# A linear-attention and expert layer on one core: second gate and router with fewer TensorE passes, a norm moved, eight blocks a body

## What is computed

```python
x = x + attention(layernorm(x))          # x: (2, 8192, 512) fp32, 16384 tokens in all
x = x + experts(layernorm(x))

# attention, 16 heads of 32, chunks of 64 tokens
q, k, v = h @ Wq + bq, h @ Wk + bk, h @ Wv + bv
gate  = sigmoid(silu(h @ Wg1 + bg1) @ Wg2 + bg2)     # Wg1: (512, 16), Wg2: (16, 512)
alpha = 0.9 * gate + 0.1
intra = softmax(causal(q k^T / sqrt(32))) v          # within a chunk
inter_t = q_t S;   S = alpha_t * S + k_t v_t^T       # a state per head, token by token
out = intra + inter

# experts, 64 of them, top 8 per token, 256 slots each, and one shared expert
probs = softmax(h @ router_w.T); w = top8(probs) / sum
out = sum_e w_e * (silu(h @ w_gate[e]) * (h @ w_up[e])) @ w_down[e]
    + (silu(h @ sg) * (h @ su)) @ ws_down
```

## Time and profile before

| | |
|---|---|
| median of 3 runs | 4751.03 us |
| the profiled execution | 4743.73 us, span 4741.9 us |
| TensorE busy, matmuls | 4469.1 us (94%), 74544 instructions |
| VectorE busy | 3521.0 us (74%) |
| ScalarE busy | 2271.8 us (48%) |
| POOL busy | 1333.6 us (28%) |
| granted TensorE clock, mean | 0.983 |
| DMA | 358.52 MB, mean 76 GB/s |

### The profile page before, as it was taken

One profiled execution on the slowest core, in us unless ns is written; L12 is line 12 of the kernel. 1 busy time (PEld: TensorE's weight loads), 2 busy tenths in 40 slices (PEclk: granted clock), 3 DMA queues, 4 the chain that ended last, 5 costly groups with the idle time before them and its releaser, 6 DMA issues. The chain is left out here.

```text
span 4741.9 us, 183468 instructions
## 1 busy us (share of the span) xinstructions
PE 4469.1 (94%) x74544; PEld 3903.7 (82%) x74544; DVE 3521.0 (74%) x7639; ACT 2271.8 (48%) x7475; POOL 1333.6 (28%) x1272
## 2 busy tenths in 40 slices
PE   6999999999999999999999999999999959999998
PEld 5888888888888888888888888888888859999998
DVE  5777777777777777777777777777777768888887
ACT  4444444444444444444444444444444436666665
POOL 2111111111111111111112121212111146666666
PEclk9999999999999999999999999999999979999999
DMA  2000000001000000000000000000000069999997
GB/s 65 31 31 31 31 33 28 36 31 36 31 31 31 31 31 31 31 31 31 31 31 31 31 31 31 31 31 34 28 35 31 31 193 269 267 266 267 269 270 194
DMA packets 195054, 358.52 MB, mean 76 GB/s; under 512 B 16736, under 2 KB 92896, under 8 KB 194352
## 3 DMA queue, kind: packets, MB, share of 16 engines
q1 hardware_dynamic: 160848, 269.47, 16.8%
q0 software_dynamic: 33632, 79.73, 7.6%
HBM read 243.87 MB, written 107.50 MB: 74 GB/s over the span
## 5 line engine op out<-in xcount | busy, mean ns | idle before, releaser
L583 ACT ACTIVATE PR<-PR,MX 128x64 f32<-128x64 f32 x2048 | 682.6, 334 | 808.1 <-DVE MX L1159 808.1
L469 POOL TENSOR_TENSOR RI<-PV,AL 128x512 f32<-128x512 f32 x65 | 78.8, 1212 | 2575.2 <-DVE PV L1113 2575.2
L721 PE MATMUL bank<-XTh,wsguh 128*128 128x256 f32 x1536 | 448.1, 292 | 0.0
L1651 PE MATMUL ebank<-XH,WH 128*128 128x256 f32 x1536 | 431.3, 281 | 6.9 <-DVE XL L1733 6.9
L722 PE MATMUL bank<-XTl,wsguh 128*128 128x256 f32 x1536 | 430.8, 280 | 0.0
L723 PE MATMUL bank<-XTh,wsgul 128*128 128x256 f32 x1536 | 430.6, 280 | 0.0
L1651 PE MATMUL ebank<-XH,WL 128*128 128x256 f32 x1536 | 429.7, 280 | 0.0
L1651 PE MATMUL ebank<-XL,WH 128*128 128x256 f32 x1536 | 429.5, 280 | 0.0
L1726 DVE TENSOR_TENSOR WL<-WS,WH 128x768 fp32r<-128x768 f32 (+1 forms) x455 | 370.8, 839 | 16.2
L583 ACT ACTIVATION_READ_ACCUMULATOR PR<-PR,MX 128x1 f32 x2048 | 382.5, 187 | 0.0
L1588 ACT ACTIVATE WH<-WS 128x768 fp32r<-128x768 f32 (+1 forms) x455 | 325.2, 747 | 26.1 <-DMA WS<-in_L_ffn_w_down_dram 26.1
(11 more groups left out here) (228 smaller groups left out, 13542.2 us busy)
## 6 DMA issues: line engine op xcount, KB each, us to landing
WS<-in_L_ffn_w_gate_dram SPq DMA_DIRECT2D x65, 768.0 KB
WS<-in_L_ffn_w_up_dram SPq DMA_DIRECT2D x65, 768.0 KB
WS<-in_L_ffn_w_down_dram SPq DMA_DIRECT2D x65, 768.0 KB
norm_rows<-XR SPq DMA_DIRECT2D x64, 576.0 KB, 3.2
X<-in_L_attn_x_dram SPq DMA_DIRECT2D x66, 512.0 KB, 3.6
out_dram<-X SPq DMA_DIRECT2D x64, 512.0 KB, 2.9
CR<-token_counts,count_at POOLq DMA_INDIRECT x136
XG<-norm_rows,row_at POOLq DMA_INDIRECT x132
```

What stands on the lines that cost most here:

```text
L469: nc.gpsimd.tensor_tensor(inverse[:, :, 0:half], PV[:, :, :], running[:, :, HC:half:-1], ALU.mult).then_inc(folded.sem, 1)
L583: ins = nc.scalar.activation(PR[b][:, j, :], PR[b][:, j, :], ACT.Exp, bias=MX[b][:, j:j + 1], scale=1.0, accum_out=SU[b][:, j:j + 1])
L721: nc.tensor.matmul(out, sh, mh, start=first, stop=False)
L1651: last = nc.tensor.matmul(bank[HID[m]][:, a * CAP:(a + 1) * CAP], w, x[odd][:, c, :], start=(c == 0 and i == 0), stop=(c == KC - 1 and i = ...
```

## The change

The second gate's operands are stacked. Wg1 and bg1 are loaded three times, to columns 0, 32 and 64 of the padded 128, so that s1 comes out in three copies. ScalarE rounds all of s1 to sg (`s1_high`), and VectorE overwrites rows 32 to 63 of sg with the low part (`s1_low`). wg2 holds the high part of Wg2 in rows 0 and 32 and its low part in row 64 on. One f32r matmul over the 128 rows then sums high x high, low x high and high x low.

The router's weights lie side by side, high and low, in 128 columns (rwT). Four matmuls multiply them by XTh, with 128 rows of result, and four multiply the high part by XTl on top of the first 64. The logits move to SBUF with 128 rows, and the turn is an fp32 matmul with fold_ident, two identities one above the other, which adds the halves.

x is now loaded twice per block: to a single X for the norm, and to one of two X2 buffers, where the residual, the sum and the store take place. The norm of block t+2 stands in the middle of each list, and xt of block t+2 ahead of the router. The orders of scores(3), turn_probs(2), outputs(2) and the value chunks change, as do those of the first gate and the silu against the softmax. TensorE's body holds eight blocks. The diff, cut to its core:

```diff
-        wg2 = sb("wg2", [GP, DIM])
-        rwT = [sb(f"rwT{i}", [P, KC, E], f32r) for i in "hl"]
+        wg2 = sb("wg2", [GP, DIM], f32r)
+        rwT = sb("rwT", [P, KC, 2 * E], f32r)
+        fold_ident = sb("fold_ident", [P, E])
...
-        X = [sb(f"X{i}", [P, NT, DIM]) for i in range(2)]
+        X = sb("X", [P, NT, DIM])
...
+        sg = sb("sg", [GP, TB], f32r)
...
-        X2 = sb("X2", [P, NT, DIM])
+        X2 = [sb(f"X2{i}", [P, NT, DIM]) for i in range(2)]
...
-        LT = sb("LT", [E, TB])
+        LT = sb("LT", [2 * E, TB])
...
-        stages = [QT[0], QT[1], KT[0], KT[1], QD, KD, V, X2, KTok, RI, XN]
+        stages = [QT[0], QT[1], KT[0], KT[1], QD, KD, V, X2[1], KTok, RI, XN]
...
+        wg2_f = OTs[0][:, :, :].rearrange("p a b -> p (a b)")
...
-        WEIGHT_DMAS = 8
+        WEIGHT_DMAS = 5 + 3 * len(COPIES)
...
             def load_x(t):
-                sp.dma_start(X[t.buf][:, :, :], x_rows[t.pair * 2 + t.odd, :, :, :]).then_inc(x_loaded.sem, 16)
+                sp.dma_start(X[:, :, :], x_rows[t.pair * 2 + t.odd, :, :, :]).then_inc(x_loaded.sem, 16)
+
+            def load_x2(t):
+                sp.dma_start(X2[t.buf][:, :, :], x_rows[t.pair * 2 + t.odd, :, :, :]).then_inc(x2_loaded.sem, 16)
...
+            for at in COPIES:
+                sp.dma_start(wg1_f[:, :, at:at + GH], Wg1.rearrange("(c p) n -> p c n", p=P)).then_inc(weights_in, 16)
+                sp.dma_start(wg2_f[at:at + GH, :], Wg2).then_inc(weights_in, 16)
+                sp.dma_start(b1[at:at + GH, :], bg1.rearrange("(p o) -> p o", o=1)).then_inc(weights_in, 16)
...
-            load_x(Turn(0, 1))
+            load_x2(Turn(0, 0))
+            for t in (Turn(0, 0), Turn(0, 1)):
+                sp.wait_ge(xn_ready.sem, t.value(xn_ready))
+                load_x(t.next())
+            sp.wait_ge(w_low, len(staged) + 2)
...
-            def turn(t, last):
-
-                sp.wait_ge(x2_ready.sem, t.value(x2_ready))
-                if last:
-
-                    sp.dma_start(X[t.buf][:, :, :], x_rows[0, :, :, :]).then_inc(x_loaded.sem, 16)
-                else:
-                    load_x(Turn(t.pair, t.odd + 2))
+            def turn(t, more=True, x=3):
+
+                if more:
+                    sp.wait_ge(out_stored.sem, t.value(out_stored, back=1))
+                    load_x2(t.next())
+                if x is not None:
+                    sp.wait_ge(xn_ready.sem, t.next(2).value(xn_ready))
+                    load_x(Turn(t.pair, t.odd + x))
                 sp.wait_ge(rows_ready.sem, t.value(rows_ready))
                 sp.dma_start(norm_rows[t.pair * 2 + t.odd, :, :, :], XR[:, :, :]).then_inc(rows_stored.sem, 16)
                 sp.wait_ge(out_ready.sem, t.value(out_ready))
-                sp.dma_start(out_rows[t.pair * 2 + t.odd, :, :, :], X2[:, :, :]).then_inc(out_stored.sem, 16)
+                sp.dma_start(out_rows[t.pair * 2 + t.odd, :, :, :], X2[t.buf][:, :, :]).then_inc(out_stored.sem, 16)
                 sp.wait_ge(counts_ready.sem, t.value(counts_ready))
                 sp.dma_start(block_counts[t.pair * 2 + t.odd, :, :], CT[t.buf][:, :]).then_inc(counts_stored.sem, 16)
...
-            nc.gpsimd.memset(wg2[:, :], 0.0)
+            nc.gpsimd.memset(wg2_f, 0.0)
...
+            link(nc.gpsimd.memset(fold_ident[:, :], 0.0))
+            for h in range(2):
+                link(nc.gpsimd.affine_select(out=fold_ident[h * E:(h + 1) * E, :], in_=fold_ident[h * E:(h + 1) * E, :],
+                                             compare_op=ALU.not_equal, fill=1.0, base=0, pattern=[[-1, E]],
+                                             channel_multiplier=1))
...
                     fold(t.next())
                     decayed_k(t.next())
                     rstd2(t, 0)
+                    rstd1(t.next(2))
+                    rstd2(t, 1)
                     decayed_q(t.next())
-                    rstd2(t, 1)
-                    rstd1(t.next(2))
...
+            def s1_high(t):
+                act.wait_ge(s1_made.sem, t.value(s1_made))
+                act.wait_ge(g2_filled.sem, t.value(g2_filled, back=1))
+                nc.scalar.activation(sg[:, :], s1[:, :], ACT.Copy).then_inc(s1h_ready.sem, 1)
...
-                nc.scalar.activation(LT[:, :], bank_of("RL")[0:E, 0:TB], ACT.Copy).then_inc(lt_ready.sem, 1)
+                nc.scalar.activation(LT[:, :], bank_of("RL")[:, 0:TB], ACT.Copy).then_inc(lt_ready.sem, 1)
...
+            nc.scalar.activation(wg2[:, :], wg2_f, ACT.Copy).then_inc(rw_ready, 1)
...
                 for odd in range(2):
                     t = Turn(pair, odd)
                     n = t.next()
+                    gate1(n)
                     exp(t, 0)
-                    gate1(n)
+                    s1_high(n)
                     q_evac(n, 0)
                     gate2(n, 0)
                     gate2(n, 1)
                     q_evac(n, 1)
                     ot(t, 1)
                     exp(t, 3)
+                    ot(t, 2)
                     k_evac(n, 1)
-                    ot(t, 2)
                     ot(t, 3)
+                    normalise(t.next(2))
                     x2t(t)
                     ktok_evac(n, 0)
                     lt(t)
                     ktok_evac(n, 1)
                     gu(t, 0)
                     hidden_high(t, 0)
-                    normalise(t.next(2))
                     router_exp(t)
                     gu(t, 1)
                     hidden_high(t, 1)
...
-                    last = nc.tensor.matmul(b[:, a * TB:(a + 1) * TB], wg2[:, m * P:(m + 1) * P], s1[:, :], start=True, stop=True)
+                    last = nc.tensor.matmul(b[:, a * TB:(a + 1) * TB], wg2[:, m * P:(m + 1) * P], sg[:, :], start=True, stop=True)
...
                 b = take("RL", t, JOBS)
                 for c in range(KC):
                     if c % 2 == 0:
+                        pe.wait_ge(x2h_ready.sem, t.value(x2h_ready, c // 2))
+                    nc.tensor.matmul(b[:, 0:TB], rwT[:, c, :], XT[0][:, c, :], start=(c == 0), stop=(c == KC - 1))
+                for c in range(KC):
+                    if c % 2 == 0:
                         pe.wait_ge(x2l_ready.sem, t.value(x2l_ready, c // 2))
-                    last = split_product(b[0:E, 0:TB], both(rwT, ALL, c, ALL), both(XT, ALL, c, ALL), c == 0, c == KC - 1)
+                    last = nc.tensor.matmul(b[0:E, 0:TB], rwT[:, c, 0:E], XT[1][:, c, :], start=False, stop=(c == KC - 1),
+                                            skip_group_check=True)
                 last.then_inc(rl_filled.sem, 1)
             def turn_logits(t):
                 pe.wait_ge(lt_ready.sem, t.value(lt_ready))
                 apart(pe, pe_apart)
                 for tile in range(NT):
-                    last = nc.tensor.transpose(b[:, tile * E:(tile + 1) * E], LT[:, tile * P:(tile + 1) * P], ident[0:E, 0:E])
+                    last = nc.tensor.matmul(b[:, tile * E:(tile + 1) * E], LT[:, tile * P:(tile + 1) * P], fold_ident[:, :], start=True,
+                                            stop=True)
                 last.then_inc(rlt_filled.sem, 1)
...
-            with nc.Fori(0, NBLK // 2, 2, engines=[pe.engine], hint_back_edge=True) as pair:
-                for odd in range(4):
+            with nc.Fori(0, NBLK // 2, 4, engines=[pe.engine], hint_back_edge=True) as pair:
+                for odd in range(8):
                     t = Turn(pair, odd)
                     turn_probs(t, 1)
                     project(t, 1, wq, q_filled, ("Qa", "Qb"), parts=(1,))
                     outputs(t, 1)
+                    scores(t, 3)
+                    turn_probs(t, 2)
                     project(t, 1, wk, k_filled, ("Ka", "Kb"), parts=(0,))
-                    scores(t, 3)
                     turn_out(t, 0)
-                    values(t, 0, chunks=(0,))
-                    turn_probs(t, 2)
+                    values(t, 0, chunks=(0, 1))
+                    outputs(t, 2)
                     project(t, 1, wk, k_filled, ("Ka", "Kb"), parts=(1,))
-                    outputs(t, 2)
-                    values(t, 0, chunks=(1,))
                     turn_probs(t, 3)
                     values(t, 0, chunks=(2,))
                     outputs(t, 3)
                     values(t, 0, chunks=(3,))
                     turn_out(t, 1)
-                    values(t, 1, chunks=(0, 1))
+                    values(t, 1)
                     x2t(t, 0)
-                    values(t, 1, chunks=(2, 3))
                     x2t(t, 1)
                     ktok(t, 0)
+                    xt(t.next(2), 0)
+                    xt(t.next(2), 1)
                     router(t)
                     ktok(t, 1)
                     gate_up(t, 0)
                     turn_logits(t)
                     gate_up(t, 1)
-                    xt(t.next(2), 0)
-                    xt(t.next(2), 1)
                     gate_up(t, 2)
                     down(t, 0, (0, 1))
                     state_updates(t, 0)
...
```

(60 more changed lines are left out.)

14 lines of the change are left out of this document (5 added, 9 removed).

## The result

The changed kernel takes 4814.82 us (median of 4 runs, 4811.43 to 4837.19) against 4750.07 us (median of 4 runs): ratio 1.0152, interval 1.0136 to 1.0169. It is 1.5% slower; 3.2% faster was forecast. The span of the profiled execution is 4809.5 us, 67.6 more than before, and all of it lies in the token loop: from block 0 to block 63 it is 3741.7 us instead of 3674.0, and block 0 itself is only 1.7 us later.

The account below looks back on a forecast made before the run. The prediction took TensorE's instruction stream in the token loop, plus its back edges, as the bound. From 4743.7 us: -110 inside blocks, -43.5 for edges, +6 before the loop gives 4596, plus 4: 4600 us, range 4535 to 4670.

Parts of the forecast that it names:

- What bounds the kernel: Token loop: TensorE busy in 3512 of 3674 us, ordinary periods near 56.7 us, 62.83 us across a back edge.
- body of eight: TensorE's loop: 15 back edges become 7, eight turning into ordinary turn-rounds, -43.5 us (-24 to -56).
- Norm in mid-block: Norm of block t+2 fills VectorE's idle time, decayed_q goes behind both roots; x2's transposes end 0.7 us sooner.
- Scores(3) before the k projection: Mid-block: softmax_a(3) starts 0.6 us sooner, raising TensorE's gain in a block from 0.3 to 0.6 us.
- rival D: Rival, chance 0.04: the added 512 KB load of x holds up TensorE's instruction fetch in each block, 390 us, 4990 us.
- Second gate: Early in the block: 1.33 us less TensorE work, 0.69 us won, 0.64 paid for a new wait; VectorE's stretch shrinks it.
- Router: Late in the block: 12 matmuls become 8, 1.17 us gained, with the logits' turn costing 0.14 us more.
- rival B: Rival, chance 0.10: VectorE's stretch takes back the gain inside a block, 4666 us; sign: second-gate wait over 1.5 us.
- Ahead of the loop: Before the loop: six more small loads on SP take 6.6 us to issue, +6 us (+3 to +10).
- walk through the block: One ordinary block followed in the new order: period 54.8 instead of 56.6 us, 1.75 taken, -110 us over 63.
- A: Rival, chance 0.09: instruction cost goes by amount, not by edge, so the body of eight stops as long, 4643 us.
- C: Rival, chance 0.03: every wait closes and only the work remains, 4.3 us gained a block, 4440 us.

Follow-up runs that it names:

- e4: Kernel before with only TensorE's loop body changed, from four blocks to eight: 4701.75 us, ratio 0.9908 to the kernel before.
- e1: Changed kernel with one added wait, so POOL starts decayed_q only after x2's second tile is normalised: 4652.07 us, ratio 0.9808 to the kernel before.
- e2: Changed kernel with TensorE's old order, scores(3) again behind half of the k projection: 4771.85 us.
- e5: e1 with TensorE's old order as well, scores(3) again behind half of the k projection: 4613.32 us, ratio 0.9716 to the kernel before.
- e7: e5 with the second gate put back to fp32, 8 matmul instructions, no rounded copy or subtraction: 4563.27 us, ratio 0.9611 to the kernel before.
- e9: e5 with eight semaphore increments more per block on TensorE, ahead of the second gate's first wait: 4588.03 us, ratio 0.9665.
- e8: e5 with the router and the logits' turn put back as in the kernel before: 4649.54 us.
- e3: Changed kernel with TensorE's loop body put back from eight blocks to four: 4850.38 us.
- e10: e5 with the residual's load of x cut to 4 columns of one tile, so only its time counts: 4612.76 us.
- e11: e7 with the changed kernel's order of scores(3), turn_probs(2) and outputs(2): 4614.76 us.

## Why the prediction was wrong

- **What bounds the kernel, edges, body of eight: right.** 5.4 us an edge, -43.5 us forecast, -45 measured (e4).
- **Norm in mid-block: the step that failed.** I wrote that decayed_q "goes behind both" roots and "isn't read before the next block's scores", and took that as its cost: none. I asked who waits for decayed_q, not what runs beside it. In the order before, POOL starts it just after VectorE has begun the first tile's normalising, and is through ahead of the second's; the new list starts it just ahead of the second. VectorE's 0.55 us become 2.2, TensorE waits 1.7 us in each of the 63 periods (105 us), and 29 of them lose 1.6 us to the clock (46 us). In all 163 us (e1), which is more than the whole forecast gain.
- **Scores(3) before the k projection: wrong in sign.** Of the 0.3 us a block that I walked 0.2 are there (even periods 54.98 with it, 55.18 without), but the dense run of small matmuls outruns the instructions in the odd periods: -39 to -43 us for undoing it (e2, e5). The sum had no term for this. I had looked for waits on data only; my rival D had the right resource and the wrong cause and place.
- **Second gate: the walk was nearly right, its worth wrong.** Work saved 1.3 us by the forecast (1.0 in the even periods' busy time, e7 against e5), wait 0.9, VectorE takes the rest back; then 50 us are lost at edges and in odd periods (e7), half of which eight idle instructions give back (e9). What the other half is stays open.
- **Router: 36 us** (e8), 0.57 us a block, where rival B put its part at 0.7. **Ahead of the loop:** +1.7 us, not +6; the six added small loads took 3.0 us to issue, not the 6.6 that the durations of the earlier trace rows gave, and TensorE's first work came 2.9 us later. The 1.7 us are hardly told from nothing: block 0 comes at 132.96 us in the kernel before and at 134.44 in e4, with the same code ahead of the loop.
- **The sum.** Without the hold and with the old order the kernel takes 4613 us, 13 above the forecast, with periods of 55.2, 55.9 and 62.4 us where 54.9, 55.6 and 61 were forecast: the walk through the block was good as a whole. Part of that is luck, because the gate's loss of 50 us, which it hadn't, is made up by other parts. The forecast failed on two resources that it did not walk, the neighbour on POOL and the instruction supply. None of the rivals was what happened: A falls with e3 and e4, D with e10, the gate's wait stayed below B's sign, and C had every wait close. The range excluded what happened, because I gave 0.04 to all slower cases.

The version that beats both kernels is e7: 4563 us, 3.9% below the kernel before.

## What to carry to other kernels

When an instruction moves in one engine's list, look at what the engine beside it will run at the same time, not only at who waits for whom: VectorE's tensor_scalar and a product on POOL didn't run side by side in any of these kernels, and the one that started second paid what was left of the first: up to 0.3 us for POOL in one order, 1.7 us for VectorE in the other. A pass saved on TensorE is worth what the next wait leaves of it, and an undone edit on top of a repaired kernel shows that better than a sum. A long run of tiny matmuls did better here with large ones in its middle, and a change in a loop's code length shifted 25 us by itself, so a difference of that size needs a padded control.

## What the runs showed of the hardware

- A VectorE tensor_scalar of 128x512 fp32 from SBUF to SBUF: 0.55 us alone, 2.2 us when POOL's product of 128x1024 starts ahead of it; one of 128x2: 0.17 and 0.83 us. In the other order POOL's product is the longer one: 2.47 us where it starts 0.13 us behind VectorE's, 2.2 alone.
- 160 small matmul instructions with their weight loads in about 3 us came with a stop of 1.1 to 1.8 us for instructions in 19 of 24 odd periods and in none of the even ones of the changed kernel; with the fp32 gate (e11) stops of 0.8 to 1.6 us stood in 12 odd and 14 even ones.
- Such a stop ended 1.2 to 1.6 us behind the landing of a 16384-byte packet of the instruction queue in all 23 cases in the changed kernel's blocks; the one shown took 1.20 us.
- Behind stops of TensorE of 1.1 to 1.7 us the granted clock fell from 1.00 to the lower level (1.2 GHz) in part of the cases; 12 matmuls of 256 columns then took 2.6 us instead of 1.4.
- Eight semaphore increments more per block moved the period across a back edge from 62.4 to 59.6 us.
